# Sparse top-32 cross-attention: the output projection of a pair of batches in four parts, with two buffers for its turned sums

## The chip, the cores and the metric

One Trainium2 chip, one core of it. The metric is the device time of one execution in microseconds; of three runs of the kernel before, the median is given. The program has twelve stages that follow one another; the change touches one, the cross-attention of layer 3.

## What is computed

The model is a small Perceiver with 16 batches, 64 latent rows of 128 numbers each, and a context of 1601 rows per batch. In the stage at issue each latent row attends with 16 heads of width 8 over the 1601 context rows, keeps the 32 highest scores, and adds the result to `x`:

```python
x = x + _L3_xattn_ref(_layernorm(x, axis=-1), ctx_1024, Wq, bq, Wk, bk, Wv, bv, Wo, bo)

scores = jnp.einsum('bhsd,bhnd->bhsn', Q, K) / SCALE          # 16 batches, 16 heads, 64 x 1601
topk_scores, topk_indices = jax.lax.top_k(scores, 32)
sparse_weights = jax.nn.softmax(topk_scores, axis=-1)
context = jnp.einsum('bhsk,bhskd->bhsd', sparse_weights, sel_V)
context = context.transpose(0, 2, 1, 3).reshape(B, S, D_MODEL)
return context @ Wo.T + bo
```

## The kernel before

**Tiles.** `topk_cross_attention` works in 128 tiles, `t` = 0 to 127. A tile is one batch and two heads: 2 x 64 = 128 rows of 1601 scores. `TB` = 8 tiles make a batch, 16 tiles (`2 * TB`) a pair of batches, and there are `NT` = 8 pairs. `x` is stored by pairs: `x[:, p, :]` has the 128 rows of pair `p`.

**What happens to a tile**, and on which engine:

- TensorE: `scores(t)` multiplies queries and keys into `psS` (L912). `turn(t, q)` turns the weights P by 128x128 blocks into `psT` (L922), `values(t, q)` multiplies them with the raw context into `psU` (L934), `turn_u(t)` turns the 128x128 result into the first 128 columns of `psZ` (L945).
- ScalarE (ACT): `copy_scores` copies `psS` to `SS` (L993), `negate` and `exps` make exponentials (L999, L1006), `count_sides` compares with the 32nd value (`sides`, L1018, and `listed_sides`, L1022), `mark` makes the 0/1 weights P in two passes (L1031, L1034), `copy_weights` copies `psT` to `PT` (L1042), `norm` scales `psU` into `U` (L1050), `copy_ut` copies `psZ` to `UT` (L1058).
- VectorE (DVE): `fold` pairs the two halves of the scores (L1143 and L1145), `find` and `drop` take the top 32 in four rounds of eight (L1159, L1164), `invert_span` (L1172) and `inverse` (L1178) are reciprocals of one column.
- GpSimd (POOL): `equal_span`, `weigh` (small sums, L1106 to L1120, then P times the exponentials, L1124).

**Keys.** In the tiles named in `keyed`, t = 8b+1 to 8b+4, the keys of the next batch are made as well, one block of 512 columns at a time (the fourth has 65): TensorE L901, and ACT copies the block (`keys`, L986). These are the first tiles of each batch after its very first.

**The output of a pair.** When the 16 tiles of pair `p` are through, `UT` holds all 16 heads turned, 128x128 each. `sums(p)` then multiplies each with its block of `N` (value and output weights already multiplied together) and adds up 16 products in columns 128 to 255 of `psZ` (L950; a 32-bit product appears as two MATMUL records). `add(p)` on DVE adds these to `x` (L1182). `psZ` has 512 32-bit columns.

**Order.** Each engine runs a loop over steps `s`, and the order within a step is written out by hand. In step `s`, TensorE does `scores(s+1)`, then for t = s-2 the key block, `turn(t,0)`, `turn(t,1)`, `turn_u(t-1)`, `turn(t,2)`, `turn(t,3)`, `values(t,0..3)`, and if t is a multiple of 16 above 0, `sums` of the pair just finished. So `sums` stands between `values(t)` and `scores(s+2)`. ACT in step `s` does `count_sides(s-1)`, `copy_scores(s+1)`, `norm(s-3)`, `keys`, `copy_weights(s-2, 0 and 1)`, `mark(s-1)`, `copy_weights(s-2, 2 and 3)`, `negate`, `exps`, and last `copy_ut(s-3)`. DVE in step `s` does three operations of find and drop, `inverse(s-3)`, `add` where it is due, `drop`, `invert_span(s-1)`, `find`, `fold(s+1, high)`, `drop`, `fold(s+1, low)`, `find`. The fold reads `psS` directly and the copy in `SS`, so it waits for `copy_scores(s+1)`; the next `scores` waits until both folds have read `psS`.

`sums(p)` waits for `ut_ready` (the copy of the tile before, which is last in ACT's step), `turn_u` at t = 16, 32, ... waits for `y_added`, and `copy_ut` at these tiles waits for `y_ready`, as there is one `UT`.

Of the kernel before, what the change touches and what calls it, by code (L numbers as in the profile page):

```python
# [14 lines left out]
B, S, D = 16, 64, 128  # L15
NT = B * S // 128
# [3 lines left out]
H = 16  # L20
# [6 lines left out]
ONE = 1  # L27
# [755 lines left out]
def topk_cross_attention(c, N, QT, WkT, bk):  # L783
# [3 lines left out]
    TB = H // 2  # L787
    T = B * TB
# [2 lines left out]
    LOW = -3.0e38  # L791
    TOPK = 32
    LISTS = 7
    with ExitStack() as st:
        ctxT = c.sb(st, "ctxT", [128, 2, K])
        ctxN = c.sb(st, "ctxN", [128, 2, NC, D + 4])
# [16 lines left out]
        li = c.sb(st, "li", [128, 2])  # L813
        ones = c.sb(st, "ones", [128, 1])
        U = c.sb(st, "U", [128, 2, D])
        UT = c.sb(st, "UT", [128, H, 2, S])
        psS = c.ps(st, "psS", [128, 2048])
        psT = c.ps(st, "psT", [128, 2, 512])
        psU = c.ps(st, "psU", [128, 512])
        psZ = c.ps(st, "psZ", [128, 512])  # L820
# [4 lines left out]
        for t in range(T):  # L825
            if t in keyed:
                uses.append(("keys", *keyed[t]))
            uses += [("weights", t, q) for q in range(4)]
        slot = {use: u for u, use in enumerate(uses)}

        loaded = [c.sem("ctx_loaded0"), c.sem("ctx_loaded1")]
        turned_loaded = [c.sem("ctxT_loaded0"), c.sem("ctxT_loaded1")]
# [9 lines left out]
        u_turned, ut_ready = c.sem("u_turned"), c.sem("ut_ready")  # L842
        y_ready, y_added = c.sem("y_ready"), c.sem("y_added")
# [13 lines left out]
        with nc.Block() as block:  # L857
# [24 lines left out]
            @block.tensor  # L882
            def _(pe):
                def bank_free(use):
                    u = slot[use]
                    if u >= 2:
                        kind, a, n = uses[u - 2]
                        if kind == "keys":
                            pe.wait_ge(kt_ready, BLOCKS * a + n + 1 + ONE)
                        else:  # L890
                            pe.wait_ge(pt_ready, 4 * a + n + 1 + ONE)
                    return u % 2

                def project(b, n):
                    o, w = KB[n]
                    pe.wait_ge(turned_loaded[b % 2], 16 * (b // 2 + 1) + ONE)
                    if b == 0:
                        keys = psS[:, o:o + w]
                    else:
                        keys = psT[:, bank_free(("keys", b, n)), 0:w]  # L900
                    pe.matmul(keys, WkT, ctxT[:, b % 2, o:o + w], start=True, stop=True).then_inc(kp_ready, 1)  # L901

                def scores(t):
                    b, n = t // TB, t % TB
                    if n == 0:
                        pe.wait_ge(kt_ready, BLOCKS * (b + 1) + ONE)
                        pe.wait_ge(stat_ready, b + 1 + ONE)
                    if t:
                        pe.wait_ge(copied, t + ONE)
                        pe.wait_ge(folded, 2 * t + ONE)  # L910
                    for o, w in KB:
                        last = pe.matmul(psS[:, o:o + w], stat[:, b % 2, 2 * n:2 * n + 2, :], KT[:, b % 2, o:o + w],  # L912
                                         start=True, stop=True)
                    last.then_inc(scored, 1)

                def turn(t, q):
                    if q == 0:
                        pe.wait_ge(p_ready, t + 1 + ONE)
                    j = bank_free(("weights", t, q))
                    for k in range(4 * q, min(4 * q + 4, NC)):  # L920
                        o, w = KC[k]
                        last = pe.transpose(psT[0:w, j, (k % 4) * 128:(k % 4) * 128 + 128], P[:, t % 2, o:o + w],  # L922
                                            c.ident[:])
                    last.then_inc(turned, 1)

                def values(t, q):
                    if q == 0:
                        pe.wait_ge(loaded[t // TB % 2], 32 * (t // TB // 2 + 1) + ONE)
                    if q == 0 and t:
                        pe.wait_ge(us_ready, t + ONE)  # L930
                    pe.wait_ge(pt_ready, 4 * t + q + 1 + ONE)
                    for k in range(4 * q, min(4 * q + 4, NC)):
                        w = KC[k][1]
                        last = pe.matmul(psU[:, 0:D + 1], PT[0:w, t % 2, k, :], ctxN[0:w, t // TB % 2, k, 0:D + 1],  # L934
                                         start=(k == 0), stop=(k == NC - 1))
                    if q == 3:
                        last.then_inc(u_ready, 1)

                def turn_u(t):
                    pe.wait_ge(us_ready, t + 1 + ONE)  # L940
                    if t:
                        pe.wait_ge(ut_ready, t + ONE)
                    if t % (2 * TB) == 0 and t:
                        pe.wait_ge(y_added, t // (2 * TB) + ONE)
                    pe.transpose(psZ[:, 0:128], U[:, t % 2, :], c.ident[:]).then_inc(u_turned, 1)  # L945

                def sums(p):
                    pe.wait_ge(ut_ready, 2 * TB * (p + 1) + ONE)
                    for h in range(H):
                        last = pe.matmul(psZ[:, 128:256], UT[:, h, :, :], N[:, h, :], start=(h == 0),  # L950
                                         stop=(h == H - 1))
                    last.then_inc(y_ready, 1)

                for n in range(BLOCKS):
                    project(0, n)
                scores(0)
                for s in range(T + 2):
                    if s + 1 < T:
                        scores(s + 1)
                    t = s - 2  # L960
                    if t in keyed:
                        project(*keyed[t])
                    if t >= 0:
                        turn(t, 0)
                        turn(t, 1)
                    if t >= 1:
                        turn_u(t - 1)
                    if t >= 0:
                        turn(t, 2)
                        turn(t, 3)  # L970
                        for q in range(4):
                            values(t, q)
                        if t and t % (2 * TB) == 0:
                            sums(t // (2 * TB) - 1)
                turn_u(T - 1)
                sums(NT - 1)

            @block.scalar
            def _(act):
# [15 lines left out]
                def negate(t):  # L995
                    act.wait_ge(listed, LISTS * t + 1 + ONE)
                    if t >= 2:
# [11 lines left out]
                def count_sides(t):  # L1009
                    j = t % 2  # L1010
                    edge = top[:, j, TOPK - 1:TOPK]
                    act.wait_ge(listed, LISTS * (t + 1) + ONE)
                    if t:
# [39 lines left out]
                def copy_ut(t):  # L1053
                    p, b, n = t // (2 * TB), t // TB, t % TB
                    act.wait_ge(u_turned, t + 1 + ONE)
                    if t % (2 * TB) == 0 and p:
                        act.wait_ge(y_ready, p + ONE)
                    act.activation(UT[:, 2 * n:2 * n + 2, b % 2, :],  # L1058
                                   psZ[:, 0:128].rearrange("p (h s) -> p h s", s=S), ACT.Copy).then_inc(ut_ready, 1)

                for n in range(BLOCKS):
# [73 lines left out]
            def _(dve):  # L1135
                def fold(t, low):
# [3 lines left out]
                    if t >= 2:  # L1140
                        dve.wait_ge(listed, LISTS * (t - 1) + ONE)
                    if low:
# [34 lines left out]
                        dve.wait_ge(us_ready, t - 1 + ONE)  # L1177
                    dve.reciprocal(li[:, t % 2:t % 2 + 1], psU[:, D:D + 1]).then_inc(li_ready, 1)  # L1178

                def add(p):  # L1180
                    dve.wait_ge(y_ready, p + 1 + ONE)
                    dve.tensor_tensor(c.x[:, p, :], c.x[:, p, :], psZ[:, 128:256], ALU.add).then_inc(y_added, 1)  # L1182

                fold(0, False)
# [1 line left out]
                for s in range(T + 2):  # L1186
                    if s < T:
                        find(s, 0, HALF)
                        drop(s, 0, HALF)
                        find(s, 1, HALF)  # L1190
                    if s >= 3:
                        inverse(s - 3)
                        if s > 3 and (s - 3) % (2 * TB) == 0:
                            add((s - 3) // (2 * TB) - 1)
                    if s < T:
                        drop(s, 1, HALF)
                    if 0 <= s - 1 < T:
                        invert_span(s - 1)
                    if s < T:
                        find(s, 2, KP)  # L1200
                    if s + 1 < T:
                        fold(s + 1, False)
                    if s < T:
                        drop(s, 2, KP)
                    if s + 1 < T:
                        fold(s + 1, True)
                    if s < T:
                        find(s, 3, KP)
                inverse(T - 1)
                add(NT - 1)  # L1210
                dve.wait_ge(y_added, NT + ONE)


def stage_l3_xattn(c):
# [2277 lines left out]
```

## Time and profile before

| | us |
|---|---|
| median of 3 runs | 4617.7 |
| lowest, highest | 4614.1, 4618.28 |
| the profiled execution | 4626.02 |
| span of its trace | 4623.5 |
| PE busy | 3563.3 (77%) |
| DVE busy | 3459.4 (75%) |
| ACT busy | 2800.4 (61%) |
| POOL busy | 1031.0 (22%) |
| L950 (`sums`) MATMUL, 256 records | 42.0 |
| L1182 (`add`), 8 instructions | 2.3 |

The span is that of all twelve stages, from the first to the last instruction. Busy shares are averages over stages with different limits, so they say little about one of them. The tiles of the stage at issue run from about 2840 to 4325 us of the span; what is read below comes from there. A line number is a line of the kernel before.

### The profile page before, as it was taken

The numbers are of one execution on the slowest core, as the hardware profiler recorded it, in microseconds if no ns is written. First come the engines' busy times: TensorE is split into PE (matmuls) and PEld (weight loads), VectorE is DVE, ScalarE is ACT, GpSimd is POOL, SyncE is SP. The second block draws the span as 40 slices with busy tenths as digits, with TensorE's granted clock in tenths as the row PEclk, the third lists the DMA queues.
The fourth block names the chain that finished last, engine by engine and source line by source line (L and its number), as shares of the span: only waits on it lengthen the run. The fifth ranks groups of instructions, "written<-read, shape, count | busy, mean of one in ns | idle before, by whom it ended". The sixth has DMA issues, their size and how long they took to land. (4 is left out here: it accounts for less than half of the span.)

```text
span 4623.5 us, 71954 instructions
## 1 busy us (share of the span) xinstructions
PE 3563.3 (77%) x25855; PEld 2857.9 (62%) x25855; DVE 3459.4 (75%) x5612; ACT 2800.4 (61%) x4626; POOL 1031.0 (22%) x1050
## 2 busy tenths in 40 slices
PE   6345617999999777999999876777777777777776
PEld 3234305999999555899999743555555555555664
DVE  4675786787877622877787657999999999999433
ACT  3113504666666422666666425998989999889422
POOL 0000402111120201121111102444444434434200
PEclk9556758999999888999999888999999999999877
DMA  8543001010110101010110001000000000000000
GB/s 275 86 74 86 6 0 62 29 44 29 37 37 15 25 23 61 30 43 30 37 37 22 22 8 36 15 29 15 15 15 29 15 15 15 17 20 1 20 3 16
DMA packets 186564, 161.24 MB, mean 35 GB/s; under 512 B 8220, under 2 KB 174316, under 8 KB 186220
## 3 DMA queue, kind: packets, MB, share of 16 engines
q1 hardware_dynamic: 179564, 140.38, 11.0%
q10 hardware_dynamic: 6656, 16.38, 1.2%
q8 instruction: 202, 3.31, 0.3%
q14 instruction: 142, 1.16, 0.1%
HBM read 127.36 MB, written 20.20 MB: 32 GB/s over the span
## 5 line engine op out<-in xcount | busy, mean ns | idle before, releaser
L537 PEld LDWEIGHTS psU<-ctxN,ST 128*128 128x128 f32 x6656 | 853.0, 191 | 97.6 <-issue 39.1
L537 PE MATMUL psU<-ctxN,ST 128*128 128x129 f32 x6656 | 867.0, 276 | 20.4 <-issue 20.4
L1159 DVE MAX8 top<-pairs 128x8 f32<-128x801 f32 (+1 forms) x512 | 709.2, 1406 | 4.8 <-issue 0.3
L623 ACT ACTIVATE ST<-ST 128x512 f32<-128x512 f32 (+1 forms) x832 | 513.2, 625 | 165.2 <-DVE ST L725 161.1
L934 PE MATMUL psU<-ctxN,PT 128*128 128x129 f32 (+1 forms) x3328 | 433.5, 282 | 201.8 <-ACT PT L1042 201.8
L1124 POOL TENSOR_TENSOR P<-P,EX 128x1601 f32<-128x1601 f32 x128 | 459.7, 3591 | 570.8 <-ACT P L1034 570.8
L725 DVE TENSOR_TENSOR ST<-ST,psB 128x512 f32<-128x512 f32 (+1 forms) x832 | 556.1, 677 | 2.8 <-PE psB L556 2.8
L711 DVE TENSOR_TENSOR psA<-psA,ST 128x512 f32<-128x512 f32 x640 | 446.7, 698 | 137.2 <-ACT ST L615 69.7
L934 PEld LDWEIGHTS psU<-ctxN,PT 128*128 128x128 f32 (+1 forms) x3328 | 395.7, 194 | 226.1 <-ACT PT L1042 226.1
L1164 DVE MATCH_REPLACE8 pairs<-top,pairs 128x801 f32<-128x801 f32 (+1 forms) x384 | 482.4, 1256 | 0.0
L912 PE MATMUL psS<-KT,stat 128*128 128x512 f32 (+1 forms) x1024 | 386.1, 520 | 15.9 <-DVE pairs L1143 15.1
L525 PE MATMUL psS<-statL,ctxH 128*128 128x512 f32 x832 | 393.9, 473 | 5.6 <-ACT ST L615 2.7
L615 ACT ACTIVATE ST<-psS,key_bias 128x512 f32<-128x512 f32 (+1 forms) x416 | 283.9, 682 | 144.9 <-PE psS L525 139.8
L618 ACT ACTIVATE ST<-psS 128x512 f32<-128x512 f32 (+1 forms) x416 | 246.5, 592 | 166.9 <-PE psS L525 162.1
L922 PE MATMUL psT<-ident,P 128*128 128x128 f32 (+1 forms) x1664 | 256.6, 283 | 97.1 <-ACT KT L986 71.8
L525 PE MATMUL psS<-statH,ctxH 128*128 128x512 f32 x832 | 330.7, 397 | 0.0
L525 PE MATMUL psS<-statH,ctxL 128*128 128x512 f32 x832 | 327.7, 394 | 0.0
L912 PEld LDWEIGHTS psS<-KT,stat 128*128 128x128 f32 x1024 | 189.6, 195 | 208.9 <-issue 207.9
L922 PEld LDWEIGHTS psT<-ident,P 128*128 128x128 f32 (+1 forms) x1664 | 192.7, 144 | 167.3 <-ACT KT L986 86.0
L655 POOL CAST ctxH<-ctxM 128x1601 fp32r<-128x1601 f32 x30 | 45.6, 1520 | 1011.5 <-DVE ctxM L684 1011.5
L1042 ACT ACTIVATE PT<-psT 128x512 f32<-128x512 f32 (+1 forms) x512 | 240.0, 509 | 18.7 <-PE psT L922 18.7
L993 ACT ACTIVATE SS<-psS 128x1601 f32<-128x1601 f32 x128 | 192.2, 1502 | 76.5 <-PE psS L912 76.1
(509 smaller groups left out, 6361.9 us busy)
## 6 DMA issues: line engine op xcount, KB each, us to landing
ctxT<-ctxT_scratch SPq DMA_DIRECT2D x48, 800.5 KB, 4.6
ctxN<-in_ctx SPq DMA_DIRECT2D x48, 768.0 KB
ctxT_scratch<-trn ACTq DMA_DIRECT2D x16, 800.5 KB
nat<-in_ctx SPq DMA_DIRECT2D x16, 768.0 KB
ctx<-in_ctx SPq DMA_DIRECT2D x16, 768.0 KB
dist_scratch<-dd SPq DMA_DIRECT2D x8, 800.5 KB
room<-dcol SPq DMA_DIRECT2D x28, 201.0 KB, 4.2
dcol<-dist_scratch SPq DMA_DIRECT2D x16, 201.0 KB, 17.0
```

The lines of the kernel that those rows point to most:

```text
L525: last = pe.matmul(psS[:, i % RING, :], x[:, u // 2 % 2, o:o + 128], q[:, p % 2, heads, queries], start=(n_pass == 0), stop=(n_pass == 2))
L537: last = pe.matmul(psU[:, q, 0:D + 1], ST[0:n, i % SLOTS, q * 128:q * 128 + 128], ctxN[0:n, j, k, 0:D + 1], start=(k == 0 and q % 2 == 0), ...
L615: act.activation(ST[0:n, i % SLOTS, :], psS[0:n, i % RING, :], ACT.Identity, bias=key_bias[0:n, col:col + 1]).then_inc(copied, 1)
L623: act.activation(ST[0:n, i % SLOTS, :], ST[0:n, i % SLOTS, :], ACT.Exp).then_inc(exp_done, 1)
L711: dve.tensor_tensor(psA[:], psA[:], cell, ALU.max).then_inc(folded, 1)
L725: dve.tensor_tensor(cell, cell, psB[0:n, :], ALU.subtract).then_inc(shifted, 1)
L912: last = pe.matmul(psS[:, o:o + w], stat[:, b % 2, 2 * n:2 * n + 2, :], KT[:, b % 2, o:o + w], start=True, stop=True)
L922: last = pe.transpose(psT[0:w, j, (k % 4) * 128:(k % 4) * 128 + 128], P[:, t % 2, o:o + w], c.ident[:])
L934: last = pe.matmul(psU[:, 0:D + 1], PT[0:w, t % 2, k, :], ctxN[0:w, t // TB % 2, k, 0:D + 1], start=(k == 0), stop=(k == NC - 1))
L1124: pool.tensor_tensor(P[:, j, :], P[:, j, :], EX[:, j, :], ALU.mult).then_inc(p_ready, 1)
L1159: dve.max(top[:, j, 8 * n:8 * n + 8], pairs[:, j, 0:width]).then_inc(listed, 1)
L1164: dve.match_replace(pairs[:, j, 0:width], top[:, j, 8 * n:8 * n + 8], pairs[:, j, 0:width], LOW).then_inc(listed, 1)
```

## The change

`UT` gets a second buffer, so that a pair's turned sums can be kept while those of the next are written. The output of a pair is then made in four parts of four heads each, in tiles t = 16(p+1)+1 to 16(p+1)+4, one part per tile, and no longer all in tile 16(p+1). Each part is its own accumulation in `psZ`, and is added to `x` by its own `add`. Waits change with it: a part waits for `ut_ready` of its own tile and for the part before it to be added; `turn_u` in these four tiles waits for the part's `y_added`; `copy_ut` at the first tile of a pair waits for the sums of two pairs before. For the last pair the four parts follow each other at the end.

```diff
+    PARTS = 4
+    PAIR = 2 * TB
-        UT = c.sb(st, "UT", [128, H, 2, S])
+        UT = c.sb(st, "UT", [128, 2, H, 2, S])
+        summed = {PAIR * (p + 1) + 1 + g: (p, g) for p in range(NT - 1) for g in range(PARTS)}
 def turn_u(t):
-                    if t % (2 * TB) == 0 and t:
-                        pe.wait_ge(y_added, t // (2 * TB) + ONE)
+                    if t in summed:
+                        p, g = summed[t]
+                        pe.wait_ge(y_added, PARTS * p + g + 1 + ONE)
-                def sums(p):
-                    pe.wait_ge(ut_ready, 2 * TB * (p + 1) + ONE)
-                    for h in range(H):
-                        last = pe.matmul(psZ[:, 128:256], UT[:, h, :, :], N[:, h, :], start=(h == 0),
-                                         stop=(h == H - 1))
+                def sums(p, g, t):
+                    pe.wait_ge(ut_ready, t + ONE)
+                    n = PARTS * p + g
+                    if n:
+                        pe.wait_ge(y_added, n + ONE)
+                    heads = range(g * H // PARTS, (g + 1) * H // PARTS)
+                    for h in heads:
+                        last = pe.matmul(psZ[:, 128:256], UT[:, p % 2, h, :, :], N[:, h, :], start=(h == heads[0]),
+                                         stop=(h == heads[-1]))
                     last.then_inc(y_ready, 1)
-                        if t and t % (2 * TB) == 0:
-                            sums(t // (2 * TB) - 1)
+                        if t in summed:
+                            sums(*summed[t], t)
                 turn_u(T - 1)
-                sums(NT - 1)
+                for g in range(PARTS):
+                    sums(NT - 1, g, T)
 def copy_ut(t):
-                    if t % (2 * TB) == 0 and p:
-                        act.wait_ge(y_ready, p + ONE)
-                    act.activation(UT[:, 2 * n:2 * n + 2, b % 2, :],
+                    if t % PAIR == 0 and p >= 2:
+                        act.wait_ge(y_ready, PARTS * (p - 1) + ONE)
+                    act.activation(UT[:, p % 2, 2 * n:2 * n + 2, b % 2, :],
-                def add(p):
-                    dve.wait_ge(y_ready, p + 1 + ONE)
+                def add(p, g):
+                    n = PARTS * p + g
+                    dve.wait_ge(y_ready, n + 1 + ONE)
+                    if n:
+                        dve.wait_ge(y_added, n + ONE)
                     dve.tensor_tensor(c.x[:, p, :], c.x[:, p, :], psZ[:, 128:256], ALU.add).then_inc(y_added, 1)
-                        if s > 3 and (s - 3) % (2 * TB) == 0:
-                            add((s - 3) // (2 * TB) - 1)
+                        if s - 3 in summed:
+                            add(*summed[s - 3])
```

## Rows read from the trace of the kernel before

**Rows 1.** Busy time by stretch, the tiles of the stage; columns in the first line.

```profile
core 0: us, PE busy (x) PEld busy (x) DVE busy (x) ACT busy (x) POOL busy (x), PEclk, DMA share, GB/s
2840.00:4325.00 1485.00, 1107.44 (x6498) 810.86 (x6496) 1419.62 (x1795) 1352.96 (x1972) 608.13 (x650) 0.98 0.05 16
```

**Rows 2.** Waits of DVE, same stretch: total us, times, longest.

```profile
DVE x L1182 <- PE psZ L950: 20.1, 8, 5.0
...
DVE inv_span L1172 <- POOL span L1109: 13.4, 22, 3.1
DVE pairs L1145 <- ACT SS L993: 8.2, 7, 1.2
```

**Rows 3.** Timeline, two plain tiles: start, us, engine, line, operation, [idle before, releaser].

```profile
3105.95 0.15 DVE L1178 RECIPROCAL li<-psU 128x1 f32<-128x1 f32 x1
...
3113.46 0.26 ACT L1058 ACTIVATE UT<-psZ 128x128 f32<-128x128 f32 x1
...
3114.35 1.63 ACT L1018 ACTIVATE sides<-SS,top 128x1601 f32<-128x1601 f32 x1 [0.63 <-DVE top L1159]
...
3116.28 1.48 ACT L993 ACTIVATE SS<-psS 128x1601 f32<-128x1601 f32 x1
...
3117.25 0.15 DVE L1178 RECIPROCAL li<-psU 128x1 f32<-128x1 f32 x1
...
3120.20 0.97 DVE L1145 TENSOR_TENSOR pairs<-psS,SS 128x801 f32<-128x801 f32 x1
```

**Rows 4.** Timeline of the tile in which the first pair is summed (t = 16).

```profile
3031.21 1.62 ACT L1018 ACTIVATE sides<-SS,top 128x1601 f32<-128x1601 f32 x1
...
3031.37 3.84 PE L950 MATMUL psZ<-N,UT 128*128 128x128 f32 x32 [0.69 <-ACT UT L1058]
...
3033.82 0.15 DVE L1178 RECIPROCAL li<-psU 128x1 f32<-128x1 f32 x1
...
3035.04 2.91 PE L912 MATMUL psS<-KT,stat 128*128 128x512 f32 x8
...
3035.24 0.29 DVE L1182 TENSOR_TENSOR x<-x,psZ 128x128 f32<-128x128 f32 x1 [1.28 <-PE psZ L950]
...
3037.99 1.51 ACT L993 ACTIVATE SS<-psS 128x1601 f32<-128x1601 f32 x1 [4.76 <-PE psS L912]
...
3039.53 0.99 DVE L1145 TENSOR_TENSOR pairs<-psS,SS 128x801 f32<-128x801 f32 x1 [1.17 <-ACT SS L993]
```

**Rows 5.** Timeline of the four key tiles after it (t = 17 to 20).

```profile
3049.55 1.51 ACT L993 ACTIVATE SS<-psS 128x1601 f32<-128x1601 f32 x1 [0.22 <-PE psS L912]
...
3050.08 0.17 DVE L1172 RECIPROCAL inv_span<-span 128x1 f32<-128x1 f32 x1 [1.02 <-POOL span L1109]
...
3058.88 1.62 ACT L1018 ACTIVATE sides<-SS,top 128x1601 f32<-128x1601 f32 x1
...
3061.12 1.50 ACT L993 ACTIVATE SS<-psS 128x1601 f32<-128x1601 f32 x1 [0.23 <-PE psS L912]
...
3072.69 1.51 ACT L993 ACTIVATE SS<-psS 128x1601 f32<-128x1601 f32 x1 [0.23 <-PE psS L912]
...
3081.64 1.62 ACT L1018 ACTIVATE sides<-SS,top 128x1601 f32<-128x1601 f32 x1
...
3083.89 1.51 ACT L993 ACTIVATE SS<-psS 128x1601 f32<-128x1601 f32 x1 [0.23 <-PE psS L912]
...
3092.27 1.62 ACT L1018 ACTIVATE sides<-SS,top 128x1601 f32<-128x1601 f32 x1
```

**Rows 6.** Timeline: TensorE where its granted clock fell, `sums` twice and `scores` once.

```profile
3215.92 5.47 PE L950 MATMUL psZ<-N,UT 128*128 128x128 f32 x32 [0.69 <-ACT UT L1058]
...
3401.61 6.59 PE L950 MATMUL psZ<-N,UT 128*128 128x128 f32 x32 [0.49 <-ACT UT L1058]
...
3124.30 3.91 PE L912 MATMUL psS<-KT,stat 128*128 128x512 f32 x5
```

**Rows 7.** Timeline: the last pair's sums and their addition.

```profile
4316.45 3.84 PE L950 MATMUL psZ<-N,UT 128*128 128x128 f32 x32 [0.37 <-ACT UT L1058]
...
4320.33 0.29 DVE L1182 TENSOR_TENSOR x<-x,psZ 128x128 f32<-128x128 f32 x1 [5.03 <-PE psZ L950]
```

More of the change, by code:

```diff
@@ L1209, in _ @@
                 inverse(T - 1)
-                add(NT - 1)
-                dve.wait_ge(y_added, NT + ONE)
+                for g in range(PARTS):
+                    add(NT - 1, g)
+                dve.wait_ge(y_added, PARTS * NT + ONE)
 def stage_l3_xattn(c):
```

## The prediction

> **What bounds the kernel now.** I read three views, in this order: busy time by stretch, the waits of the engine that the first one points to, and the timeline of single tiles. Over the tiles of the stage DVE is busy 1419.6 of 1485.0 us, ACT 1353.0, PE 1107.4 [rows 1]: DVE sets the pace and ACT is close behind it. A plain tile takes 11.29 us from one `inverse` to the next (3105.95 to 3117.25, like most of the 128), and there ACT waits 0.63 us for DVE before `sides` [rows 3]. What DVE loses is in its waits [rows 2]: for the sums of a pair 20.1 us, of which 5.0 are the last pair's; for `span` 13.4, of which 3.1 fall at the end of the stage; for the copied scores 8.2. With the seven additions of 0.29 us the seven inner pairs cost 15.1 + 10.3 + 8.2 + 2.0 = **35.6 us**, 5.1 per pair. That is all that the change can touch inside the stage.
>
> Rows 4 show how these 5.1 us arise. PE waits 0.69 us for `copy_ut`, which is last in ACT's step; the 16 heads then hold it 3.67 us (3031.37 to 3035.04); so `scores` is late, ACT stands idle 4.76 us before it can copy them, and DVE waits for the sums (1.28) and for the copy (1.17). ACT is now behind. In the next tile DVE waits 1.02 us for `span`, which hangs on ACT's `sides` [rows 5].
>
> **The limit in the four tiles after it.** The reader should look at the starts of ACT's score copy: 3049.55, 3061.12, 3072.69, 3083.89 [rows 5]. They are 11.57 us apart, more than DVE's 11.29, and before each ACT waits 0.23 us for PE. This is a loop through two engines: score copy, key copy, weights, `exps`, `copy_ut`, `sides` on ACT; `values`, `scores` on PE. In tiles that also make keys it has no room at all. The change puts its four parts in just these tiles.
>
> **The change part by part.**
>
> Removed: the block of 16 heads in tile 16(p+1), with its waits: 35.6 us in total.
>
> Added to the loop: four times a part. Its cost is read from the block. The 32 records take 3.67 us until `scores` starts, 0.115 each [rows 4], so 8 records take 0.92. From `sides` to the score copy it was 3037.99 - 3031.21 = 6.78 us with 32 records [rows 4]; with 24 fewer it is 6.78 - 2.75 = **4.03**. From score copy to the next `sides` ACT needs 3058.88 - 3049.55 = 9.33 us in a key tile, 3081.64 - 3072.69 = 8.95 in the fourth, whose key block is short, and 3092.27 - 3083.89 = 8.38 in a plain one [rows 5]. So the loop takes 9.33 + 4.03 = 13.36 us for the first three parts and 8.95 + 4.03 = 12.98 for the fourth, together 53.06 us, where DVE alone wants four times 11.29.
>
> The lead that ACT has at the start: in a plain tile the copy starts 0.97 us before `inverse` (3116.28 against 3117.25), and the fold, which needs its result 1.54 us after its start (3037.99 to 3039.53), comes 2.95 us after `inverse` [rows 3, 4]. After four parts the copy starts at -0.97 + 53.06 = 52.09 us after the first `inverse`, and its fold at 53.63; undisturbed it would be at 4 x 11.29 + 2.95 = 48.11. DVE has lost 5.5 us. In the next, plain tile ACT needs 8.38 us to `sides`, and DVE, which can invert the span 2.8 us after that, loses some 0.15 us more. Sum: **5.7 us per pair**, 39.6 for seven, which is 4.0 more than is removed. The short reason: today one wait of 0.69 and one block of 3.67 stand in the loop, 4.36 us; afterwards four waits of 0.69 and four blocks of 0.92, 6.4 us; and ACT's lead is used up once either way, since the tiles between the parts give nothing back.
>
> The wait for `copy_ut` is a price from rows 4 (0.69) and rows 6 (0.69, 0.49). The data of part g have been ready since the pair ended, but `sums` waits for the copy of its own tile. Here a rule of the Trainium skill speaks against the change: PSUM — Partial Sum Buffer, section "PSUM bank collisions raise a hardware error", says that two engines must not be at one bank together, even in different columns, so that waits go by bank. `psZ` is one bank by its size, so by this rule the wait belongs to every part. Without it the seven pairs would be 7 x 4 x 0.69 = 19.3 us cheaper; the trace agrees that the one block waits, and shows no part without a wait.
>
> Additions: four of 0.29 us for one, 0.87 us more per pair on DVE, 6.1 us in total. They cost nothing as long as DVE waits for the copied scores, which it does here from the second part on; they lie in the 5.5 us. If ACT had a lead they would cost the 6.1 in full. The wait in front of each is short, as a part ends about 1.3 us after `sides`; behind it `drop` and the rest of DVE's step are queued, which have to wait for the late scores anyway. The Trainium skill (Perfetto Trace Analysis, "Optimizing Scalar/DVE Operations") says that each DVE instruction on PSUM carries about 125 ns of its own, so that grouping pays on a full engine: three more instructions would be an estimated 0.38 us per pair by that page, against 0.87 by the row; both are covered.
>
> `turn_u` waits for the addition in four tiles instead of one. It comes after two `turn`s and after ACT's `norm`, which itself follows `inverse`; the addition directly follows `inverse` too. Between 0 and 0.3 us each, taken as 0. `copy_ut` no longer waits for the sums of the pair before; it did not wait visibly, so 0. The second buffer has no cost in time. DMAs are not touched.
>
> The end of the stage: one block of 3.84 us, 0.04 to the addition, 0.29 for it, 4.17 in all [rows 7]. Then four times a block of 8 records, 3.84 - 24 x 0.115 = 1.08, with the two hand-overs and the addition: about 1.45, so 5.8. Cost **+1.7** us; up to +3 if TensorE is at the lower clock.
>
> **The clock.** At its lower level (1.2 instead of 2.4 GHz) the block of 3.84 us took 5.47 and 6.59 [rows 4, 6]; it was stretched in six of the seven inner pairs, by 0.95 to 2.75. The rows before it show what PE did: it had stood idle for `PT` and then waited for `copy_ut` again. This is already in the 35.6. Afterwards these two idle stretches come back in four tiles per pair. A stretch of 3.4 us at the lower level costs 5.47 - 3.84 = 1.6 us, on `scores` about as much (5 records took 3.91 us where 8 take 2.91) [rows 4, 6], and in these tiles nothing hides it. Bounds: no drop, 0 us; one in each of the four tiles, 6.5 us per pair. I take one per pair, the commonest count today: 7 x 1.65 = **+11.6** us.
>
> Sum: -35.6 + 39.6 + 1.7 + 11.6 = **+17.3 us**. Against the profiled execution: span 4623.5 to 4641, its own time 4626.0 to 4643. The median of the runs is 8.3 us under that time; the same sum on it gives 4617.7 + 17.3 = **4635 us**.
>
> **The rivals.**
>
> *The clock stays up.* Fewer columns in one block, work spread out: PE might not drop at all. Then -35.6 + 39.6 + 1.7 = +5.7, 4623 us. For it: plain key tiles show no drop in this trace. Against it: they lack the second idle stretch before the part.
>
> *Two or more drops per pair.* At least +5.7 + 23.1 = +28.8, 4646 us and more. The four tiles look alike, so what happens in one may happen in its neighbours.
>
> *The parts are hidden, so it gets faster.* If ACT and PE had room for 0.92 us in each tile, only the additions would remain: 7 x 4 x 0.29 = 8.1 instead of 35.6, +1.7 at the end: -25.8, 4592 us. The mechanism decides at one point: the loop with a part must take no more than 11.29 + 0.29 = 11.58 us. Without a part it takes 11.57 already [rows 5], which speaks against it; that ACT waits 0.63 us for DVE in a plain tile [rows 3] speaks for some room, used once.
>
> *The wait for `copy_ut` does not recur.* If PE reached the part later than the copy, each part would cost 0.92 instead of 1.61: the loops sum to 50.3, the loss is 2.9 per pair, and the total is 20.3 - 35.6 + 1.7 = -13.6 without and -2.0 with one drop, 4604 to 4616 us. Against it: `copy_ut` stands behind `exps` in ACT's queue, and `values` is done before it in rows 4 and 6.
>
> **How the numbers follow.** One drop per pair 0.42; clock stays up (or nearly) 0.25; two or more drops 0.15; hidden parts 0.08; no recurring wait 0.10. The forecast is the first case, 4635. The range goes from 4618 (no drop, and a lead somewhat greater than read) to 4652 (two to three drops). About 0.2%, 9 us, is what a measurement of this kernel can tell from no change. Slower by more: the first and third case and a few hundredths of the second, 0.64. Within: most of the second and part of the last, 0.22. Faster: 0.14.
>
> **What the profile would show.** In the four key tiles after a pair, `inverse` to `inverse` of 13.0 to 13.4 us from the second part on (over 14 with a drop), and one MATMUL row of L950 with 8 records and an idle time of 0.5 to 0.7 before it, ended by `UT`; ACT waiting about 2 us for `psS` before each copy instead of once 4.8; tile 16(p+1) at a plain 11.29. DVE's waits for the score copy should be its largest, those for the sums small. The prediction is wrong if these tiles take 11.6 us (there was room), if no idle time stands before the parts, or if drops of the clock are absent or in every tile.

## The result and the profile after

The changed kernel took **4642.1 us** (median of 5 runs, 4634.2 to 4647.0) where the kernel before took 4615.0 on the same chip: ratio 1.0054, 95% interval 1.0039 to 1.0069, so 18 to 32 us slower. In a second session, beside other experiments, it took 4636.6 against 4620.9, ratio 1.0036 (1.0022 to 1.0050). The profiled execution took 4647.0 us, its span 4645.1, where the one before had 4626.0 and 4623.5. The forecast was 4635, or 17 us slower.

The same two views as before the prediction. DVE's waits in the stage, changed kernel (engine, line, waited for: total us, times, longest); they answer to [rows 2]:

```profile
DVE pairs L1155 <- ACT SS L1003: 29.0, 22, 3.3
DVE x L1195 <- PE psZ L959: 21.5, 25, 2.3
...
DVE inv_span L1182 <- POOL span L1119: 5.3, 15, 3.1
```

The waits for the score copy have grown from 8.2 to 29.0 us and are the largest, as forecast. Those for the sums were to be small and are not: 21.5 us, a little more than the 20.1 before, of which 6.3 fall at the end of the stage and the rest in front of the inner additions, 0.25 to 1.55 us each. L959 is now `sums`, L1195 `add`, L1003 ACT's score copy, L1188 `inverse`.

Timeline of the second and third part of a pair, changed kernel (start, us, engine, line, operation, [idle before, releaser]); it answers to [rows 4, 5]:

```profile
3429.44 1.51 ACT L1003 ACTIVATE SS<-psS 128x1601 f32<-128x1601 f32 x1 [2.02 <-PE psS L916]
...
3436.84 1.38 PE L938 MATMUL psU<-ctxN,PT 128*128 128x129 f32 x10 [1.54 <-ACT PT L1052]
...
3438.77 1.62 ACT L1028 ACTIVATE sides<-SS,top 128x1601 f32<-128x1601 f32 x1
...
3438.92 1.16 PE L959 MATMUL psZ<-N,UT 128*128 128x128 f32 x8 [0.69 <-ACT UT L1068]
3439.72 0.15 DVE L1188 RECIPROCAL li<-psU 128x1 f32<-128x1 f32 x1
...
3452.19 1.62 ACT L1028 ACTIVATE sides<-SS,top 128x1601 f32<-128x1601 f32 x1
...
3452.34 1.16 PE L959 MATMUL psZ<-N,UT 128*128 128x128 f32 x8 [0.70 <-ACT UT L1068]
3452.76 0.15 DVE L1188 RECIPROCAL li<-psU 128x1 f32<-128x1 f32 x1
3453.34 2.91 PE L916 MATMUL psS<-KT,stat 128*128 128x512 f32 x8
...
3456.28 1.51 ACT L1003 ACTIVATE SS<-psS 128x1601 f32<-128x1601 f32 x1 [2.08 <-PE psS L916]
3457.82 0.99 DVE L1155 TENSOR_TENSOR pairs<-psS,SS 128x801 f32<-128x801 f32 x1 [0.96 <-ACT SS L1003]
...
3466.18 0.15 DVE L1188 RECIPROCAL li<-psU 128x1 f32<-128x1 f32 x1
```

Each part has its 0.7 us of idle time in front; ACT then waits 2.08 us for the scores and DVE 0.96 for ACT. From `sides` to `sides` it is 3452.19 - 3438.77 = 13.42 us, and `inverse` to `inverse` settles at the same 13.42 (3452.76 to 3466.18). In the pair in which the clock did not drop, the five tiles from the first part on take 11.42, 13.04, 13.42, 13.05 and 11.42 us, together 5.88 more than five plain ones; the tile 16(p+1) takes a plain 11.29.

The fourth part of the same pair, changed kernel. First TensorE alone in two stretches of 3.41 us, with the granted clock after the parenthesis (1.00 is 2.4 GHz, 0.50 is 1.2), then the timeline.

```profile
core 0: us, PE busy (x), PEclk, DMA share, GB/s
3461.88:3465.29 3.41, 1.38 (x10) 1.00 0.00 0
3465.29:3468.70 3.41, 3.31 (x10) 0.50 0.00 0
```

```profile
3465.39 1.78 PEld L959 LDWEIGHTS psZ<-N,UT 128*128 128x128 f32 x8 [0.89 <-ACT UT L1068]
3465.39 2.08 PE L959 MATMUL psZ<-N,UT 128*128 128x128 f32 x8 [0.70 <-ACT UT L1068]
...
3467.26 3.63 PE L916 MATMUL psS<-KT,stat 128*128 128x512 f32 x8
...
3470.93 1.51 ACT L1003 ACTIVATE SS<-psS 128x1601 f32<-128x1601 f32 x1 [3.68 <-PE psS L916]
3472.47 1.00 DVE L1155 TENSOR_TENSOR pairs<-psS,SS 128x801 f32<-128x801 f32 x1 [1.85 <-ACT SS L1003]
```

The first line of the timeline is the weight load of the part, which stood idle 0.89 us. The part took 2.08 instead of 1.16 us, the scores 3.63 instead of 2.91, and ACT and DVE behind them waited 1.60 and 0.89 us longer.

The end of the stage, changed kernel, timeline; answers to [rows 7]:

```profile
4339.04 1.16 PE L959 MATMUL psZ<-N,UT 128*128 128x128 f32 x8 [0.37 <-ACT UT L1068]
4340.24 0.29 DVE L1195 TENSOR_TENSOR x<-x,psZ 128x128 f32<-128x128 f32 x1 [2.35 <-PE psZ L959]
...
4340.67 1.13 PE L959 MATMUL psZ<-N,UT 128*128 128x128 f32 x8 [0.47 <-DVE x L1195]
...
4345.04 0.29 DVE L1195 TENSOR_TENSOR x<-x,psZ 128x128 f32<-128x128 f32 x1 [1.31 <-PE psZ L959]
```

From the first product to the end of the last addition it is 6.29 us; it was 4.17.

**Where the time went.** Taking all `inverse` instructions of tiles 16 to 124 in a trace and subtracting 108 x 11.2935 us (the plain tile) gives what the stage loses to the pairs; below, "loss" means this number. It is 37.3 us in the kernel before, 56.0 in the changed one and 50.9 in the second trace of it. Between the two profiled executions that is 18.7 us, and 2.1 at the end, together 20.8, where the executions differ by 21.0. A pair in which the clock did not drop in these tiles loses 5.88 us, four with one drop of 3.4 us in a tile with a part 7.2 to 8.0 (the one of 8.0 had another drop just before its parts), one with a drop of 6.8 us 8.9, and one with a drop of 6.8 and one of 3.4 us 11.2.

### The profile page after: what moved, and what is told of

Same layout as the page of the kernel before. It is cut to its first block and busy times, and to the rows that moved or that the text cites. A ratio compares the mean times of both kernels' runs of the same rounds, so it can differ in the third digit from the quotient of the medians.

```text
span 4645.1 us, 72039 instructions
## 1 busy us (share of the span) xinstructions
PE 3566.8 (77%) x25855; PEld 2853.1 (61%) x25855; DVE 3466.4 (75%) x5636; ACT 2800.2 (60%) x4626; POOL 1032.8 (22%) x1050
## 5 line engine op out<-in xcount | busy, mean ns | idle before, releaser
L1003 ACT ACTIVATE SS<-psS 128x1601 f32<-128x1601 f32 x128 | 192.4, 1503 | 103.4 <-PE psS L916 102.6
```

## The experiments

Theory A is the one of the prediction: the four parts stand in a loop through ACT and PE that has no room in the tiles that also make keys; each meets the wait for `copy_ut` again, and idle time on TensorE there also brings drops of the clock. The rivals: the further additions cost the time; the place in the step or the tile does not matter; or the wait only fills time that would be lost anyway. All times are medians of five rounds, and all kernels are edits of the changed one; diffs are against it, and three dots stand in them for what is left out. The kernel before ran 4620 to 4621 us beside them.

**Parts in tiles without keys.**

```diff
-        summed = {PAIR * (p + 1) + 1 + g: (p, g) for p in range(NT - 1) for g in range(PARTS)}
+        summed = {PAIR * (p + 1) + 5 + g: (p, g) for p in range(NT - 1) for g in range(PARTS)}
```

> The changed kernel with its four parts in tiles 16(p+1)+5 to +8, in which no keys are made, instead of +1 to +4; nothing else differs. Theory A (the loop through ACT and PE is what costs, and the key tiles have no room in it): the loop with a part takes 8.38 + 4.03 = 12.4 us instead of 13.4, so the seven pairs lose about 2.2 us each instead of 5.9 without drops of the clock: 4596 us, and 4607 with one drop per pair. Theory B (the three more additions and hand-overs per pair are what costs, wherever they stand): as the changed kernel, 4642 us.

Measured: 4649.4 us, ratio to the kernel before 1.0058 (1.0045 to 1.0072). Neither theory as written: A missed by over 40 us. `inverse` of tiles 103 to 107 in this kernel, timeline (the third and fourth part stand in tiles 103 and 104; 105 to 108 make keys):

```profile
4066.95 0.15 DVE L1188 RECIPROCAL li<-psU 128x1 f32<-128x1 f32 x1
4079.44 0.15 DVE L1188 RECIPROCAL li<-psU 128x1 f32<-128x1 f32 x1
4091.92 0.15 DVE L1188 RECIPROCAL li<-psU 128x1 f32<-128x1 f32 x1
4104.27 0.15 DVE L1188 RECIPROCAL li<-psU 128x1 f32<-128x1 f32 x1
4115.84 0.15 DVE L1188 RECIPROCAL li<-psU 128x1 f32<-128x1 f32 x1
```

The tiles with a part take 12.48 us, as the loop said (12.4). But the next ones take 12.35 and 11.57: the parts now end where the next batch's key tiles begin, and the lag that ACT has brought along is paid there. Undisturbed, such a pair loses about 5.5 us (12.48 three times, 0.3 in the first, then 1.06 + 0.28 + 0.28), hardly less than 5.9. The rest goes with the clock: between 2860 and 4280 us of the span it was at its lower level for 75.1 us, in 20 stretches, against 47.8 us in 12 in the changed kernel; the loss in this trace is 63.7 us. The loop held; what I left out is that four plain tiles give back nothing if four key tiles follow, and that the clock would fall more often there. So it was not the keys alone that made the tiles +1 to +4 a bad place.

**Parts in TensorE's gap, in the key tiles.** In each tile TensorE waits 1.5 to 1.8 us between the second and third group of values, for ACT's copies. The part goes there; ACT's copy of the turned sums waits for the part, the addition for the copy.

```diff
-                    pe.wait_ge(ut_ready, t + ONE)
+                    pe.wait_ge(ut_ready, PAIR * (p + 1) + ONE)
...
                         for q in range(4):
                             values(t, q)
-                        if t in summed:
-                            sums(*summed[t], t)
+                            if q == 1 and t in summed:
+                                sums(*summed[t], t)
...
 def copy_ut(t):
...
+                    if t + 1 in summed:
+                        a, g = summed[t + 1]
+                        act.wait_ge(y_ready, PARTS * a + g + 1 + ONE)
...
-                def add(p, g):
+                def add(p, g, t):
...
+                    dve.wait_ge(ut_ready, t + ONE)
```

> The four parts stay in the key tiles, but TensorE does each between the second and third group of values, where it waits 1.54 us for ACT's copies, and the part no longer waits for the copy of its own tile's turned sums; ACT's copy waits for the part, and the addition for the copy, since they share a PSUM bank. Theory A (0.69 us of waiting and 0.92 us of products at the end of the step are in the loop, in the gap they are not): only the additions remain, 4 x 0.29 us per pair: 4588 us. Theory B (the key tiles are full for TensorE whatever the place, or the additions cost): 4630 us or more.

Measured: 4589.0 us, ratio 0.9929 (0.9917 to 0.9942); loss 4.4 us. Theory A. The same 28 parts and 28 additions in the same tiles cost next to nothing where TensorE stands idle anyway; the rivals that the additions cost the time, and that the place in the step does not matter, have fallen. The edit takes away the wait and moves the part at once; the kernel with the copy earlier, below, separates the two.

**The same in tiles without keys** (`+ 5 + g` as above).

> As the kernel with the parts in TensorE's gap, but in tiles +5 to +8 without keys, where the gap is 1.82 us. Theory A: the same as in the key tiles or 1 to 2 us less, 4587 us, and no waits of DVE for the sums or the score copies but at the end. Theory B (place in the step does not matter, the tile does): as e1, 4596 to 4607 us.

Measured: 4587.0 us, ratio 0.9924 (0.9910 to 0.9938); loss 3.5 us. Timeline of a part in this kernel:

```profile
3481.69 1.06 PE L959 MATMUL psZ<-N,UT 128*128 128x128 f32 x8
3483.80 1.38 PE L938 MATMUL psU<-ctxN,PT 128*128 128x129 f32 x10 [1.06 <-ACT PT L1052]
3485.02 2.91 PE L916 MATMUL psS<-KT,stat 128*128 128x512 f32 x8
3485.57 0.26 ACT L1071 ACTIVATE UT<-psZ 128x128 f32<-128x128 f32 x1
3486.45 1.63 ACT L1028 ACTIVATE sides<-SS,top 128x1601 f32<-128x1601 f32 x1 [0.63 <-DVE top L1172]
...
3489.35 0.15 DVE L1191 RECIPROCAL li<-psU 128x1 f32<-128x1 f32 x1
3489.42 0.27 DVE L1199 TENSOR_TENSOR x<-x,psZ 128x128 f32<-128x128 f32 x1
...
3500.77 0.15 DVE L1191 RECIPROCAL li<-psU 128x1 f32<-128x1 f32 x1
```

The part has no idle time before it, 1.06 us are left over after it, and `scores` follows the values at once. ACT keeps its 0.63 us of lead, and DVE does not wait for the sums. The tile takes 11.42 us, 0.13 more than a plain one: that is all an addition costs.

**One block, moved out of the way.**

```diff
-    PARTS = 4
+    PARTS = 1
...
-        summed = {PAIR * (p + 1) + 1 + g: (p, g) for p in range(NT - 1) for g in range(PARTS)}
+        summed = {PAIR * (p + 1) + 5 + g: (p, g) for p in range(NT - 1) for g in range(PARTS)}
```

> One block of 16 heads per pair as in the kernel before, with the second buffer, but in tile 16(p+1)+5 instead of 16(p+1): it stands after the key tiles. Theory A (in the kernel before 1.5 us per pair are lost behind the block, because key tiles follow, in which ACT cannot catch up): 1.9 us per pair plus the clock's share of 1.9 instead of 5.2, 4605 us. Theory B (the loss is the block itself): as before, 4615 us.

Measured: 4610.6 us, ratio 0.9975 (0.9966 to 0.9983); loss 24.7 us, 3.6 in a typical pair. A: 10.3 us less than the kernel before beside it, where A had 10 (4605 against 4615). Timeline, from the tile with the block on:

```profile
3456.34 0.15 DVE L1188 RECIPROCAL li<-psU 128x1 f32<-128x1 f32 x1
3457.98 0.29 DVE L1195 TENSOR_TENSOR x<-x,psZ 128x128 f32<-128x128 f32 x1 [1.49 <-PE psZ L959]
3460.73 1.51 ACT L1003 ACTIVATE SS<-psS 128x1601 f32<-128x1601 f32 x1 [4.76 <-PE psS L916]
3470.62 0.15 DVE L1188 RECIPROCAL li<-psU 128x1 f32<-128x1 f32 x1
...
3482.03 0.15 DVE L1188 RECIPROCAL li<-psU 128x1 f32<-128x1 f32 x1
```

The tile with the block takes 14.28, as in [rows 4] (3033.82 to the next tile, 14.07), but the next takes 11.41 and not 12.35. The block costs what it did; what followed it in the key tiles is gone, 1.6 us per pair (12.35 and twice 11.57 against 11.29). In six of the seven pairs two key tiles in front of the block now take 11.54 to 11.58 us; in all six the clock had dropped in the tile 16(p+1).

**The second buffer alone** (`PARTS = 1`, offset 0: the kernel before with the buffer and the looser wait).

> The kernel before with the second buffer alone: one block of 16 heads in tile 16(p+1), copy_ut there no longer waits for it. Both theories: the wait it removes was not seen to cost anything, so as the kernel before, 4615 to 4618 us. If it were 10 us less, the buffer by itself would bring something, and the parts would cost the more.

Measured: 4620.8 us against 4620.2, ratio 1.0001 (0.9992 to 1.0010). The buffer by itself does nothing.

**Work in the idle time, for the clock.** In the tiles with a part TensorE multiplies four more blocks in the gap, which nothing reads; ACT's copy waits for them.

```diff
                         for q in range(4):
                             values(t, q)
+                            if q == 1 and t in summed:
+                                for h in range(4):
+                                    idle = pe.matmul(psZ[:, 256:384], c.ones[:], N[:, h, :], start=(h == 0), stop=(h == 3))
+                                idle.then_inc(filler, 1)
...
 def copy_ut(t):
...
+                    if t + 1 in summed:
+                        a, g = summed[t + 1]
+                        act.wait_ge(filler, PARTS * a + g + 1 + ONE)
```

> The changed kernel with work added: in the four key tiles with a part TensorE also multiplies four more blocks of ones with N into unused columns of psZ, between the second and third group of values, where it waits 1.5 us for ACT; nothing reads them. Theory A (the clock falls in these tiles because TensorE now stands idle twice there): the drops in the key tiles go, and with them 15 us: 4627 us; the undisturbed tiles keep 13.4 us. Theory B (the drops come whatever TensorE does in the gap, or cost nothing): 4642 us, or more by the added work.

Measured: 4632.8 us, ratio 1.0026 (1.0015 to 1.0038); loss 45.5 us, and two pairs at 5.85. Timeline of one tile of this kernel, TensorE (L984 is the added work):

```profile
3438.21 1.96 PE L938 MATMUL psU<-ctxN,PT 128*128 128x129 f32 x16
3440.01 1.06 PE L984 MATMUL psZ<-N,ones 128*128 128x128 f32 x8
3441.71 1.38 PE L938 MATMUL psU<-ctxN,PT 128*128 128x129 f32 x10 [0.65 <-ACT PT L1056]
3443.79 1.16 PE L959 MATMUL psZ<-N,UT 128*128 128x128 f32 x8 [0.70 <-ACT UT L1075]
3444.79 2.91 PE L916 MATMUL psS<-KT,stat 128*128 128x512 f32 x8
```

With more work the loss is 5 to 10 us smaller than in the two traces of the changed kernel. The times point the same way, +12.6 us on the kernel before instead of +27 and +16, but the interval overlaps that of the second session. In this trace no tile with a part shows `sums` longer than 1.16 us; the drops that are left stand before the parts, in five of the seven pairs, and these lose 6.5 to 7.2 us each. So the drops in the tiles with parts go when TensorE has more to do there, and they cost 5 to 10 us of the changed kernel's loss, not the whole of its excess. Whether it is the idle time or the amount of work that counts, this edit does not separate. The undisturbed tile still takes 13.4 us.

**The copy earlier in ACT's step.**

```diff
+                    if s >= 3:
+                        copy_ut(s - 3)
                     if s < T:
                         negate(s)
                         exps(s)
-                    if s >= 3:
-                        copy_ut(s - 3)
```

> The changed kernel with one edit: ACT makes the copy of the turned sums (copy_ut) before negate and exps, no longer after them, so that a part does not wait for it. Theory A (the wait of 0.69 us recurs in four tiles and stands in the loop): tiles with a part take 12.65 instead of 13.4 us, seven pairs lose 3 us less each: 4620 us with the drops of the clock as they are, 4609 if they go with the idle time. Theory B (the wait only fills time that the loop spends elsewhere): 4642 us.

Measured: 4603.6 us, ratio 0.9965 (0.9952 to 0.9977); loss 20.7 us, against 56.0 and 50.9. Further than A's 4620 and 4609. Timeline of one tile:

```profile
3439.99 1.38 PE L938 MATMUL psU<-ctxN,PT 128*128 128x129 f32 x10 [1.54 <-ACT PT L1052]
...
3441.20 1.06 PE L959 MATMUL psZ<-N,UT 128*128 128x128 f32 x8
3442.10 2.91 PE L916 MATMUL psS<-KT,stat 128*128 128x512 f32 x8
...
3445.05 1.51 ACT L1003 ACTIVATE SS<-psS 128x1601 f32<-128x1601 f32 x1 [1.12 <-PE psS L916]
```

The wait is gone, ACT waits 1.1 us for the scores instead of 2.08, and the full tile takes 12.46 instead of 13.42: 0.96 us per part, not the 0.69 of TensorE's idle time. The rows show where the rest comes from: from the last row of `values` to the part it is 1.21 us (3439.99 to 3441.20) and was 2.08 (3436.84 to 3438.92), and `scores` starts 0.90 us after the part's start and not 1.00. An undisturbed pair, the fourth, loses 2.0 instead of 5.9, 27 us in seven, and no drop of the clock falls in a tile with a part any more; the other six had one in the tile 16(p+1) or the one before and lose 2.7 to 3.3. This one edit turns the change from a loss into a gain. The wait was the largest part of what the four parts cost.

**The copy earlier, one block** (the block in tile +5 with this edit).

> One block of 16 heads in tile 16(p+1)+5, and ACT copies the turned sums before negate and exps. Theory A (the wait before a block is 0.96 us of the loop each time it is met, here once per pair instead of four times): 7 us less than the block in the plain tile without this edit, 4604 us. Theory B (it saved so much in the four parts for another reason, such as the clock): no difference, 4611 us.

Measured: 4599.8 us, ratio 0.9959 (0.9944 to 0.9973); loss 13.5 us against 24.7. The edit brings 11 us where the wait is met once per pair; I had expected 7. The two traces divide it. Without the edit the clock dropped in each of the seven pairs in the tile 16(p+1) or the one before, five or six tiles ahead of the block; with it in the first, third, fifth and seventh pair. Where it dropped in the same tile in both traces (the first, third and fifth), the tile with the block is 0.96 to 0.97 us shorter, theory A's price of the wait. In the three pairs in which it dropped only without the edit, the pair loses 1.4 us instead of 3.6. So some 7 of the 11 us are the wait and the rest goes with the drops. A drop in a plain tile adds nothing to that tile (11.29 us), but the pair is longer later on; that it uses up ACT's lead is argued and not shown. Why three pairs have no drop here was not tried.

**Two parts of eight heads in the gap, one block at the end** (`PARTS = 2`, tiles +5 and +6).

> Two parts of eight heads per pair in TensorE's gap, in tiles 16(p+1)+5 and +6, the last pair in one block. Theory A: a part of 16 records takes 2.0 us in a gap of 1.8, which ACT's lead absorbs; per pair only two additions: 4584 us, 3 us less than four parts, of which 2 are the end. Theory B (what does not fit in the gap goes into the tile, as between key tiles): 0.2 us per part more, no difference to four parts.

Measured: **4584.4 us**, ratio 0.9926 (0.9913 to 0.9940), the lowest median of all; loss 1.5 us. Every pair loses 0.21 to 0.23 us: two tiles of 11.42. What of the 2 us does not fit the gap of 1.8 us is absorbed. From four parts it differs by less than the runs can tell.

The clock did not have to stay up for this. TensorE in one of the drops of this kernel, as a stretch (columns as above) and in the timeline (L917 is `scores`):

```profile
3558.91:3562.32 3.41, 3.41 (x6) 0.50 0.60 168
```

```profile
3558.83 4.61 PE L917 MATMUL psS<-KT,stat 128*128 128x512 f32 x8
```

`scores` took 4.61 instead of 2.91 us, and the tile still 11.29. Each of the seven pairs has such a drop in the tile before 16(p+1), and in tiles 12 to 121 there are eight in all, where the kernel before has ten. What decides is not how often the clock drops, but whether it drops where the tiles can't absorb it.

**The end alone** (four parts in the gap, last pair in one block).

> The four parts in TensorE's gap in the key tiles, as before, and the last pair in one block instead of four. Theory A (each further part at the end costs its own products' first record, an addition and two hand-overs): 2.1 us less than with four at the end, 4586 us. Rival: the end is hidden behind the start of the next stage, no difference, 4588 us.

Measured: 4589.8 us, ratio 0.9936 (0.9922 to 0.9950); against 4589.0 with four at the end the runs tell nothing. In the trace the end is 4.17 us long again (4285.38 to 4289.55), 2.1 less than in the changed kernel. Inconclusive in time, clear in the trace.

**The changed kernel again.**

> The changed kernel once more, unedited, for a second trace and on the same chip as the next two. Theory A (5.9 us per pair without a drop of the clock, and about 2 us for each drop in a key tile with a part; the number of drops differs from run to run): +16 to +27 us on the kernel before, undisturbed pairs again at 5.9. If the pair without a drop differed, the sum of the loop would be wrong.

Measured: 4636.6 us (4628.0 to 4642.8), 15.8 over the kernel before; profiled execution 4630.2, loss 50.9. The pair without a drop loses 5.84 (5.88 in the first trace); four other pairs repeat their loss within 0.03. The first and the last had a drop of 6.8 us in a tile with a part in the first trace (the first another of 3.4 behind it) and one of 3.4 here; they lose 7.9 and 7.2 instead of 11.2 and 8.9.

## Why the prediction was right

- **The loop.** 13.36 us per tile with a part was forecast, 13.42 measured. Its pieces: `sides` to score copy 4.03 against 4.09 (3452.19 to 3456.28), score copy to `sides` 9.33 against 9.33 (3429.44 to 3438.77). The undisturbed pair was to lose 5.7 us and loses 5.9. The reading of [rows 5], that tiles at 11.57 us have no room, held, but "no room at all" in key tiles is said too broadly: 11.57 is what they take behind a block, a part or a drop of the clock. The other four key tiles of a pair (16(p+1)+9 to +12) take 11.29 in most pairs of the kernel before, and the plain tiles did no better as a place for the parts (4649.4).
- **The wait.** Forecast as 0.69 us in each of four tiles; it stands there 28 times. Removing it is worth more than the row shows, 0.96 us.
- **The bank.** The rule of the Trainium skill (PSUM — Partial Sum Buffer, "PSUM bank collisions raise a hardware error") asks for an order between part, copy and addition. In the kernels with the part in the gap and in the one with the earlier copy that order is kept in another place, and the idle time is gone: the rule costs a wait only if one side comes late. No run here went without the order, so what a collision would do was not tried.
- **The clock.** One drop per pair, 1.65 us each, 11.6 in total was taken; the two traces give 56.0 - 7 x 5.88 = 14.8 and 50.9 - 7 x 5.84 = 10.0. The size of a drop of 3.4 us in a tile with a part was well read: 1.4 to 1.6 us. The count was a choice between bounds that no row decided, and that it came out, seven and six drops in tiles with parts for seven pairs, is luck. The reason given for it, idle time at `PT` and then at `copy_ut`, fits only a part of the trace of the kernel before: in tiles 12 to 121 four of its ten drops lie in plain tiles, which have no wait for `copy_ut` and lost nothing by them, and three of the six at `sums` began before that wait did. The forecast also counted drops in the tiles with parts alone; those before the parts cost too (0.6 to 1.3 us per pair, the kernel with the added work).
- **The additions** were held to be covered. They are, and in the open they cost 0.13 us each and not the 0.29 of their row; "+6.1 in full" should have been 2.7. DVE's waits in front of them were called short; they sum to 15.2 us in the inner pairs. They lie within the loss of the pairs, as the loop sets the time there.
- **The end.** +1.7 forecast, +2.1 measured: a round takes 1.60 us instead of 1.45. The block takes 1.13 and not 1.08, and the hand-over from DVE back to TensorE 0.14 (4340.53 to 4340.67) where I had used the 0.04 of the other direction.
- **The rivals.** "The parts are hidden" needed tiles of 11.6 us and found 13.4; it came true only when the parts were put in the gap, at 4587 to 4589, where it had said 4592. "The wait does not recur" came true only with ACT's order changed, at 4604, the lower edge of its 4604 to 4616. "The clock stays up" had +5.7 us and never came about in full: the kernel with the added work has no drop in a tile with a part, but five before them, and +12.6.
- **What is left open.** In the first session the medians differ by 27 us, in the second by 16, in the traces by 21. The loss explains 14 to 19 us and the end 2. The forecast of 17 lies among these numbers, but they differ by as much as its whole term for the clock. The single runs of the changed kernel spread over 13 us in one session and 15 in the other, those of the kernel before over 4 and 16. The number of drops can account for part of the spread, as the two traces show; how much, I did not measure.

## What to carry to other kernels

A wait that is cheap once is dear when a block is divided: it is paid with every part, and here four short parts behind a 0.7 us wait cost more than one long block. Before work is spread over several steps, look at whether these steps can give anything back: tiles in which a loop through two engines is already as long as the tile, or which are followed by such tiles, can't. The place for small work is the idle time that its own engine already has within the step. And moving a copy one place up in another engine's hand-written order can be worth more than moving the work to other tiles: here the first turned 16 to 27 us more than the kernel before into 17 us less, and the second gained nothing. A drop of the clock is not a cost by itself either: ask whether the tile that it falls in, and those behind it, can absorb it.

## What the runs showed of the hardware

TensorE's granted clock fell to its lower level (1.2 GHz) four to twenty times in tiles 12 to 121 of each trace, for 3.4 or 6.8 us each time, though TensorE is busy for three quarters of the stage and never stood idle there for more than 1.95 us at a stretch (1.83 in most traces). Before the drop at 3465.29 us of the changed kernel it had stood idle 1.54 us until 3463.31 and then 0.70 until 3465.39, the drop beginning in the second.

Adding matmuls that nobody needs removed the drops in the tiles with parts, and the loss of the stage became 5 to 10 us smaller. Between the two traces of the changed kernel the drops fell in the same tiles almost everywhere. In the kernel with two parts in the gap each pair has a drop, and the pairs lose 0.2 us.

An addition on DVE with a row of 0.27 to 0.29 us lengthened its tile by 0.13 us where DVE set the pace.
